# A perceiver layer on one core: x loaded four groups ahead, and stage 3 with its low-rank sums, y norm and splits in another order

## The chip, the cores and the metric

The kernel runs on one core of a Trainium2 chip. The metric is the device time of one execution in microseconds. TensorE is called PE here, VectorE DVE, ScalarE ACT, GpSimd POOL and SyncE SP, as in the rows of the profile.

## The reference

`x` is 128 batches of 32 tokens with 256 channels, `ctx` 128 batches of 257 rows with 256 channels. Three blocks follow each other, each added to `x`:

```
hc = layernorm(x)                                  # cross attention
Sim = hc @ w1 + ctx @ w2 + (hc * w3) @ ctx^T + b;  hq = softmax(Sim) @ ctx
hb = softmax(max_j Sim) @ hc                       # one row per batch
x = x + [hc, hq, hc*hq, hc*hb] @ W_qv + b_qv

z = layernorm(x); xg = z * sigmoid(z @ Wg^T + bg)  # recurrence over the 32 tokens
s = s @ A + xg * Bp;  y = s . Cp + Dp * xg + xg    # state of 16 per channel
x = x + (layernorm(y) * gamma + beta)

n = layernorm(x)                                   # feed-forward, 256 -> 1024 -> 256
h = n @ ternary(w_fc)^T + gate * (n @ v^T @ fast_b^T @ u^T)
x = x + relu(h)^2 @ ternary(w_proj)^T
```

## The kernel before, in words

The 4096 tokens are 32 groups of 128 (four batches each). `resid` holds all of x in SBUF and is updated in place. All instructions of an engine are written out by hand in program order, and engines are held to each other by semaphores (`at_least`, `wait_ge`); there is no scheduler. The program has three blocks.

Stage 1 is a software pipeline over the groups. Its step for group g does three things: part a for group g (turn ctx, scores, softmax), part b for group g - 1 (attention, feature products with `W_qv`), part c for group g - 2 (x sum, second layer norm, `z`, gate, `gated`, which goes to DRAM). `bn`, `mv`, `ve`, `rstd` are the statistics of a layer norm: DVE sums, DVE aggregates, DVE adds epsilon, POOL raises to the power -0.5. In a step DVE first adds the products to x (L843), takes the statistics of that (L848), then waits for x of group g + 1 and takes its statistics (L789, in `layer_norm1`), and only then makes `nmr` (L862) from which ACT makes `z` (L635); ACT then makes `hcwT`, the last two `ctxT` copies (L603) and PE the gate turn (L540) and the scores (L571). SP issues all loads: in step g it waits for `hc_ready`, loads x of group g + 2, waits for PE's attention, loads ctx of group g + 2, stores `gated`, and in every other step loads two groups of gated tokens for the recurrence (`scan_load`). The two semaphores `x_loaded[p]` alternate with the parity of the group.

Stage 2 turns the recurrence into a product with a Toeplitz matrix and prepares the ternary weights; the change does not touch it but for the first y addition. It writes the recurrence's result y to DRAM.

Stage 3 is the feed-forward over 8 chunks of 4 groups (512 tokens). A chunk c has 8 tiles m of 128 hidden units. For a tile PE forms `fc_ps` (L1434, four products of `xn_hi`, which lies in `toeplitz`, and `xn_lo` with `fc_T`, and L1438, one of `lr_parts` with `low_out`), ACT makes `relu` (L1489), DVE squares (L1567, into `scan_x`), ACT takes the high part `sq_hi` (L1497), POOL the low part `sq_lo` (L1526), and three tiles later PE projects both (L1451). `fc_ps` has two buffers, so PE's tile m waits for the square of tile m - 2. In between lies the preparation of later chunks:

- for chunk c + 2: DVE y sums and moments (`y_sums`, `y_moments`, tiles 1 and 2), POOL `neg_mean_y` and `rstd_y` (`lower_y`, `deviation_y`, tile 3), ACT subtracts the mean (`centre_y`, L1008, tile 4), POOL multiplies by gamma (`times_gamma`, L1015, behind tiles 4 and 5), DVE scales and adds to x (`add_y`, L1023, behind tiles 6 and 7). y lies in `y_in` or `below` by the parity of the chunk.
- for chunk c + 1: DVE x sums and moments (tiles 0 and 1), POOL `rstd_x`, `neg_mean_x`, `shift_x` (tile 1), ACT `xn` (`norm_x`, L1058, tiles 2 and 3), PE turns it (`turn_in`, L1417, behind tile 4), ACT `xn_hi` (`split_hi`, tile 5), DVE `xn_lo` (`split_lo`, behind tile 5), PE the low-rank sums (`low_rank`, L1426, behind the hidden tile 7), ACT `lr_hi` (`low_rank_hi`, L1483, behind relu 7), DVE `lr_parts` (`low_rank_parts`, L1559, behind square 7). The product of `lr_parts` in tile 0 of the next chunk waits for it.

At the end of a chunk DVE scales and adds the projection in two halves (`result`, L1575 and L1578), and SP stores 512 tokens (L1404).

## Time and profile before

| | |
|---|---|
| median of 3 runs | 589.56 us (588.4 to 592.37) |
| the profiled execution | 591.37 us |
| its span | 589.6 us |
| PE busy | 501.3 us, 85% of the span |
| DVE busy | 428.4 us, 73% |
| ACT busy | 363.6 us, 62% |
| POOL busy | 334.3 us, 57% |
| the 16 DMA engines, share of hardware queue 1 | 41.5% |

All rows come from one profiled execution. Its span runs from the first to the last event; the execution's own time is 1.8 us longer. Stage 1 lasts to about 344 us, stage 2 to about 401 us, stage 3 to the end.

### The profile page before, as it was taken

What the parts mean: (1) busy time and instruction counts of PE and PEld (TensorE: products, weight loads), DVE (VectorE), ACT (ScalarE), POOL (GpSimd) and SP (SyncE); (2) the same over time, 40 slices, a digit from 0 to 9 for tenths busy, and PEclk for the clock granted to TensorE, in tenths of its full rate; (3) what the DMA queues carried; (4) which work ended last, traced back from release to release, by engine and by line L of the source; (5) the groups of instructions that cost most, each with busy time, mean ns of one, the idle gap of its engine ahead of it and who ended that gap; (6) DMA issues with size and microseconds to landing.
All of it is one profiled execution on the core that took longest, in us unless ns stands there. A gap on an engine that the chain in (4) does not pass through costs nothing. (4 is left out here: it accounts for less than half of the span.)

```text
span 589.6 us, 12951 instructions
## 1 busy us (share of the span) xinstructions
PE 501.3 (85%) x4070; PEld 420.2 (71%) x4070; DVE 428.4 (73%) x1197; ACT 363.6 (62%) x857; POOL 334.3 (57%) x424
## 2 busy tenths in 40 slices
PE   3596999999999999999998716975888988988995
PEld 2375777878787877877786506964777877877884
DVE  2589888888888878887887606943688788788643
ACT  3464767776767766776776405563846846846652
POOL 1488666675757575766665300002767767767653
PEclk9799999999999999999999957995989989989998
DMA  7543365545645475646565761546002202201102
GB/s 225 147 157 100 104 210 156 177 142 175 189 143 176 139 213 131 190 124 205 145 186 149 193 62 39 139 109 148 31 1 72 71 2 73 71 1 36 38 1 71
DMA packets 90035, 69.90 MB, mean 119 GB/s; under 512 B 49504, under 2 KB 73328, under 8 KB 89968
## 3 DMA queue, kind: packets, MB, share of 16 engines
q1 hardware_dynamic: 89968, 69.08, 41.5%
q8 instruction: 33, 0.54, 0.4%
q14 instruction: 34, 0.28, 0.1%
HBM read 55.96 MB, written 13.11 MB: 117 GB/s over the span
## 5 line engine op out<-in xcount | busy, mean ns | idle before, releaser
L1526 POOL TENSOR_TENSOR sq_lo<-scan_x,sq_hi 128x512 fp32r<-128x512 f32 x64 | 83.7, 1308 | 58.5 <-ACT sq_hi L1497 56.5
L1489 ACT ACTIVATE relu<-fc_ps,fc_square 128x512 f32<-128x512 f32 x64 | 43.9, 686 | 54.8 <-PE fc_ps L1438 54.8
L473 PE MATMUL turn_ps<-ident,ctxn 128*128 128x128 f32 x512 | 70.8, 283 | 4.3 <-DMA ctxn<-in_ctx 4.3
L1567 DVE SCALAR_TENSOR_TENSOR scan_x<-fc_ps,relu 128x512 f32<-128x512 f32 x64 | 44.0, 687 | 38.2 <-ACT relu L1489 37.5
L603 ACT COPY ctxT<-turn_ps 128x512 f32<-128x512 f32 x128 | 68.2, 581 | 5.2 <-PE turn_ps L473 5.1
L473 PEld LDWEIGHTS turn_ps<-ident,ctxn 128*128 128x128 f32 x512 | 58.6, 145 | 17.9 <-issue 13.2
L708 POOL TENSOR_TENSOR rstd<-ve,neg_half 128x1 f32<-128x1 f32 x64 | 35.3, 551 | 43.3 <-DVE ve L796 22.5
L722 POOL TENSOR_TENSOR hc_lo<-hc_probT,hc_hi 128x256 fp32r<-128x256 f32 x32 | 23.4, 730 | 56.3 <-ACT hc_hi L610 56.3
L1434 PE MATMUL fc_ps<-toeplitz,fc_T 128*128 128x512 f32 x128 | 54.1, 422 | 0.5 <-DVE scan_x L1567 0.5
L1434 PE MATMUL fc_ps<-xn_lo,fc_T 128*128 128x512 f32 x128 | 53.0, 414 | 0.0
L714 POOL TENSOR_TENSOR proj_in<-proj_in,fc_in 128x512 f32<-128x512 f32 x31 | 49.2, 1588 | 0.0
L1451 PEld LDWEIGHTS proj_ps<-proj_T,sq_hi 128*128 128x128 f32 x256 | 40.5, 195 | 5.4
L1451 PE MATMUL proj_ps<-proj_T,sq_lo 128*128 128x256 f32 x256 | 42.5, 289 | 0.3 <-POOL sq_lo L1526 0.3
L635 ACT ACTIVATE z<-resid,nmr,rstd 128x256 f32<-128x256 f32 x32 | 19.2, 600 | 37.5 <-DVE nmr L862 37.5
L1451 PE MATMUL proj_ps<-proj_T,sq_hi 128*128 128x256 f32 x256 | 41.8, 286 | 0.0
L571 PE MATMUL score_ps<-ctxT,hcwT 128*32 128x257 f32 x512 | 34.8, 389 | 6.9 <-ACT ctxT L603 6.7
L529 PE MATMUL att_ps<-ctxn,hc_probT 128*32 128x256 f32 x512 | 35.1, 393 | 5.4 <-ACT hc_probT L618 5.4
L1497 ACT CAST sq_hi<-scan_x 128x512 fp32r<-128x512 f32 x64 | 39.3, 614 | 0.3 <-DVE scan_x L1567 0.3
L1438 PE MATMUL fc_ps<-lr_parts,low_out 128*128 128x512 f32 x64 | 27.1, 424 | 13.7 <-DVE lr_parts L1559 13.7
L577 PE MATMUL gate_ps<-wgT,zT 128*128 128x256 f32 x128 | 37.0, 413 | 0.5 <-ACT zT L648 0.5
L1451 PEld LDWEIGHTS proj_ps<-proj_T,sq_lo 128*128 128x128 f32 x256 | 36.3, 195 | 0.7 <-POOL sq_lo L1526 0.7
L815 DVE TENSOR_REDUCE fc_in<-proj_in 128x32 f32<-128x512 f32 x31 | 21.2, 685 | 18.5 <-POOL proj_in L714 18.5
(188 smaller groups left out, 1413.3 us busy)
## 6 DMA issues: line engine op xcount, KB each, us to landing
ctxn<-in_ctx SPq DMA_DIRECT2D x32, 1024.0 KB, 5.3
resid<-in_x SPq DMA_DIRECT2D x32, 128.0 KB, 4.7
ctx_end<-in_ctx SPq DMA_DIRECT2D x32, 128.0 KB
gated_tokens<-gated SPq DMA_DIRECT2D x32, 128.0 KB, 5.0
out<-resid SPq DMA_DIRECT2D x8, 512.0 KB, 3.0
scan_x<-gated_tokens SPq DMA_DIRECT2D x60, 64.0 KB, 4.8
scan_tokens<-scan_x SPq DMA_DIRECT2D x4, 768.0 KB, 9.7
y_in<-scan_tokens SPq DMA_DIRECT2D x4, 512.0 KB, 4.4
```

Of the source, the lines that this page charges most:

```text
L473: mm = pe.transpose(turn_ps[b % 2][:, (c * JT + t) * P:(c * JT + t + 1) * P], ctxn[p][:, b, t, c * P:(c + 1) * P], ident[:, :])
L529: mm = pe.matmul(att_ps[b * L:(b + 1) * L, 0:D], hc_probT[p][:, 1, t, b * L:(b + 1) * L], ctxn[o][:, b, t, :], start=(t == 0), stop=(t == ...
L577: mm = pe.matmul(gate_ps[:, 0:D], zT[:, c, :], wgT[:, c, :], start=(c == 0), stop=(c == KD - 1))
L603: act.copy(ctxT[:, b, :, 0:J - 1], turn_ps[b % 2][:, :].rearrange("p (k j) -> p k j", k=KD)).then_inc(ctxT_copied, 1)
L708: pool.tensor_tensor(dst, src, neg_half[:, 0:1], ALU.pow).then_inc(made, 1)
L714: pool.tensor_tensor(v_next[:, :, :, :], a_sb[:, :, :].rearrange("p k (n m) -> p k m n", n=N), state.unsqueeze(2).broadcast_to([P, KD, N, N]),
L1434: pe.matmul(fc_ps[m % 2][:, :], fc_T[:, k, m * P:(m + 1) * P], part[:, c, k, :], start=(k == 0 and i == 0), stop=False)
L1451: mm = pe.matmul(proj_ps[c % 2][r // 2][:, (r % 2) * D:(r % 2 + 1) * D], part[:, m, r * P:(r + 1) * P], proj_T[:, m, :], start=(m == 0 and ...
L1489: act.activation(relu[m % 2], fc_ps[m % 2][:, :], ACT.Relu, scale=fc_square[:, m:m + 1]).then_inc(relu_done, 1)
L1497: act.copy(sq_hi[:, m, :], sq[m % SQ]).then_inc(sq_hi_done, 1)
L1526: pool.tensor_tensor(sq_lo[:, m, :], sq[m % SQ], sq_hi[:, m, :].bitcast(F32), ALU.subtract).then_inc(sq_lo_done, 1)
L1567: dve.scalar_tensor_tensor(out=sq[m % SQ], in0=fc_ps[m % 2][:, :], scalar=0.0, in1=relu[m % 2], op0=ALU.max, op1=ALU.mult).then_inc(sq_don ...
```

## The change

Five edits. In stage 1 x of a group is loaded four groups ahead, on four semaphores in turn. In stage 3: the y norm is done by ACT with scale and shift at once (`norm_y`), for which POOL makes `shift_y` behind `rstd_y`; gamma is multiplied behind that and DVE's addition is a plain sum of 1024 elements in one instruction. The low-rank sums of the next chunk stand ahead of hidden tile 7 on PE, `lr_hi` ahead of relu 7, `xn_lo` ahead of square 5 and `lr_parts` ahead of square 7. Gamma stands ahead of `sq_lo` of tiles 4 and 6, and y's deviation at tile 2. The last tile's projection is done by halves, its `sq_lo` by DVE, and the last chunk is stored in two halves. `x2_done` now counts one per chunk.

```diff
-            x_loaded = [sem(f"x_loaded{p}") for p in range(2)]
+            AHEAD = 4
+            x_loaded = [sem(f"x_loaded{p}") for p in range(AHEAD)]
...
+                    if g + AHEAD < GROUPS:
+                        at_least(sp, hc_ready, g + 1)
+                        load_x(g + AHEAD)
                     if inside or g + 2 < GROUPS:
-                        at_least(sp, hc_ready, g + 1)
-                        load_x(g + 2, p)
                         at_least(sp, attended, g + 1)
...
+                for g in range(2, AHEAD):
+                    load_x(g)
...
-                        at_least(dve, x_loaded[o], sixteen(base, k, -1))
+                        at_least(dve, x_loaded[(g + 1) % AHEAD], 16 * ((g + 1) // AHEAD + 1))
...
         def lower_y(pool, c):
 
-            pool.wait_ge(mv_y_done, c + 1)
-            at_least(pool, yc_done, 2 * c - 2)
+            pool.wait_ge(rstd_y_done, c + 1)
+            at_least(pool, yn_done, 2 * (c - 1))
             pool.tensor_tensor(neg_mean_y[:, :], mv_y[:, :, 0], minus_one[:, :], ALU.mult).then_inc(neg_mean_y_done, 1)
...
+            pool.wait_ge(neg_mean_y_done, c)
+            pool.tensor_tensor(shift_y[:, :], neg_mean_y[:, :], rstd_y[:, :], ALU.mult).then_inc(shift_y_done, 1)
+
+        def norm_y(act, c, h):
+
+            act.wait_ge(shift_y_done, c)
             for r in half(h):
-                ins = act.activation(y_of(c)[:, r, :], y_of(c)[:, r, :], ACT.Identity, bias=neg_mean_y[:, r:r + 1], scale=1.0)
-            ins.then_inc(yc_done, 1)
+                ins = act.activation(y_of(c)[:, r, :], y_of(c)[:, r, :], ACT.Identity, bias=shift_y[:, r:r + 1],
+                                     scale=rstd_y[:, r:r + 1])
+            ins.then_inc(yn_done, 1)
...
-        def add_y(dve, c, h):
-
-            dve.wait_ge(centred, 2 * c + h + 1)
-            dve.wait_ge(rstd_y_done, c + 1)
-            for r in half(h):
-                ins = dve.scalar_tensor_tensor(out=res(c, r), in0=y_of(c)[:, r, :], scalar=rstd_y[:, r:r + 1],
-                                               in1=res(c, r), op0=ALU.mult, op1=ALU.add)
-            ins.then_inc(x2_done, 1)
+        def add_y(dve, c):
+
+            dve.wait_ge(centred, 2 * c + 2)
+            part = resid[:, c * CH:(c + 1) * CH, :]
+            dve.tensor_tensor(part, y_of(c)[:, :, :], part, ALU.add).then_inc(x2_done, 1)
...
+                def project_last(c, m):
+
+                    pe.wait_ge(sq_hi_done, tile(c, m) + 1)
+                    pe.wait_ge(last_lo_done, 1)
+                    for h in range(2):
+                        for part in (sq_hi, sq_lo):
+                            for r in half(h):
+                                mm = pe.matmul(proj_ps[c % 2][h][:, (r % 2) * D:(r % 2 + 1) * D],
+                                               part[:, m, r * P:(r + 1) * P], proj_T[:, m, :],
+                                               start=False, stop=(part is sq_lo), skip_group_check=True)
+                        mm.then_inc(last_half, 1)
...
+                        if m == 7 and has(c, 1):
+                            low_rank(c + 1)
                         if has(c):
                             hidden(c, m)
-                        if m == 7 and has(c, 1):
-                            low_rank(c + 1)
...
+                        if m in (4, 6) and has(c, 2):
+                            times_gamma(pool, c + 2, m // 2 - 2)
+                        if tile(c, m) < CHUNKS * MT - 1:
+                            square_lo(c, m)
...
+                def last_lo(c, m):
+
+                    dve.wait_ge(sq_hi_done, tile(c, m) + 1)
+                    dve.wait_ge(proj_tile, tile(c, m) + 1 - MT)
+                    dve.tensor_tensor(sq_lo[:, m, :], sq[m % SQ], sq_hi[:, m, :].bitcast(F32), ALU.subtract
+                                      ).then_inc(last_lo_done, 1)
```

DVE in chunk 0 of stage 3, from the square of tile 3 to the x sums of the chunk behind, before the change (`scan_x` is the square, `xn_lo` `split_lo`, `resid<-y_in` the y addition):

```order
L1567 SCALAR_TENSOR_TENSOR scan_x<-fc_ps,relu 128x512 x3
L1551 TENSOR_TENSOR xn_lo<-xt_ps,toeplitz 128x512 x2
L1567 SCALAR_TENSOR_TENSOR scan_x<-fc_ps,relu 128x512
L1023 SCALAR_TENSOR_TENSOR resid<-y_in,rstd_y,resid 128x256 x2
L1567 SCALAR_TENSOR_TENSOR scan_x<-fc_ps,relu 128x512
L1559 SCALAR_TENSOR_TENSOR lr_parts<-lr_hi,minus_lo,xt_ps 128x512
L1023 SCALAR_TENSOR_TENSOR resid<-y_in,rstd_y,resid 128x256 x2
L1567 SCALAR_TENSOR_TENSOR scan_x<-fc_ps,relu 128x512
L1032 BN_STATS bn_x<-resid 128x6 x4
```

And now:

```order
L1605 SCALAR_TENSOR_TENSOR scan_x<-fc_ps,relu 128x512 x2
L1589 TENSOR_TENSOR xn_lo<-xt_ps,toeplitz 128x512 x2
L1605 SCALAR_TENSOR_TENSOR scan_x<-fc_ps,relu 128x512 x2
L1597 SCALAR_TENSOR_TENSOR lr_parts<-lr_hi,minus_lo,xt_ps 128x512
L1605 SCALAR_TENSOR_TENSOR scan_x<-fc_ps,relu 128x512
L1040 TENSOR_TENSOR resid<-y_in,resid 128x1024
L1605 SCALAR_TENSOR_TENSOR scan_x<-fc_ps,relu 128x512
L1047 BN_STATS bn_x<-resid 128x6 x4
```

`lr_parts` stood behind half of the y addition and the square of tile 7; it now stands ahead of both, and the whole addition, one instruction, behind the last square.

PE in chunk 0 at hidden tile 7 (`fc_ps`) and the low-rank sums (`xt_ps<-...,low_in`), before:

```order
L1434 MATMUL fc_ps<-toeplitz,fc_T 128x512
L1434 MATMUL fc_ps<-xn_lo,fc_T 128x512
L1434 MATMUL fc_ps<-toeplitz,fc_T 128x512
L1434 MATMUL fc_ps<-xn_lo,fc_T 128x512
L1438 MATMUL fc_ps<-lr_parts,low_out 128x512
L1426 MATMUL xt_ps<-toeplitz,low_in 128x512
L1426 MATMUL xt_ps<-xn_lo,low_in 128x512
L1426 MATMUL xt_ps<-toeplitz,low_in 128x512
L1426 MATMUL xt_ps<-xn_lo,low_in 128x512
L1451 MATMUL proj_ps<-proj_T,sq_hi 128x256 x4
L1451 MATMUL proj_ps<-proj_T,sq_lo 128x256 x4
```

And now:

```order
L1449 MATMUL xt_ps<-toeplitz,low_in 128x512
L1449 MATMUL xt_ps<-xn_lo,low_in 128x512
L1449 MATMUL xt_ps<-toeplitz,low_in 128x512
L1449 MATMUL xt_ps<-xn_lo,low_in 128x512
L1457 MATMUL fc_ps<-toeplitz,fc_T 128x512
L1457 MATMUL fc_ps<-xn_lo,fc_T 128x512
L1457 MATMUL fc_ps<-toeplitz,fc_T 128x512
L1457 MATMUL fc_ps<-xn_lo,fc_T 128x512
L1461 MATMUL fc_ps<-lr_parts,low_out 128x512
L1474 MATMUL proj_ps<-proj_T,sq_hi 128x256 x4
L1474 MATMUL proj_ps<-proj_T,sq_lo 128x256 x4
```

The four sums moved ahead of the tile's five products, so that those and the projection stand between them and the next chunk.

POOL in chunk 0 from `rstd_x` on, before (`sq_lo` is the split of a tile's square, `y_in<-y_in,gamma_all` the gamma product):

```order
L1071 TENSOR_TENSOR rstd_x<-ve_x,neg_half 128x4
L1076 TENSOR_TENSOR neg_mean_x<-mv_x,minus_one 128x4
L1079 TENSOR_TENSOR shift_x<-neg_mean_x,rstd_x 128x4
L1526 TENSOR_TENSOR sq_lo<-scan_x,sq_hi 128x512 x2
L1002 TENSOR_TENSOR neg_mean_y<-mv_y,minus_one 128x4
L1066 TENSOR_TENSOR rstd_y<-ve_y,neg_half 128x4
L1526 TENSOR_TENSOR sq_lo<-scan_x,sq_hi 128x512 x2
L1015 TENSOR_TENSOR y_in<-y_in,gamma_all 128x512
L1526 TENSOR_TENSOR sq_lo<-scan_x,sq_hi 128x512
L1015 TENSOR_TENSOR y_in<-y_in,gamma_all 128x512
L1526 TENSOR_TENSOR sq_lo<-scan_x,sq_hi 128x512 x3
```

And now:

```order
L1087 TENSOR_TENSOR rstd_x<-ve_x,neg_half 128x4
L1092 TENSOR_TENSOR neg_mean_x<-mv_x,minus_one 128x4
L1095 TENSOR_TENSOR shift_x<-neg_mean_x,rstd_x 128x4
L1563 TENSOR_TENSOR sq_lo<-scan_x,sq_hi 128x512
L1082 TENSOR_TENSOR rstd_y<-ve_y,neg_half 128x4
L1017 TENSOR_TENSOR neg_mean_y<-mv_y,minus_one 128x4
L1019 TENSOR_TENSOR shift_y<-neg_mean_y,rstd_y 128x4
L1563 TENSOR_TENSOR sq_lo<-scan_x,sq_hi 128x512 x2
L1033 TENSOR_TENSOR y_in<-y_in,gamma_all 128x512
L1563 TENSOR_TENSOR sq_lo<-scan_x,sq_hi 128x512 x2
L1033 TENSOR_TENSOR y_in<-y_in,gamma_all 128x512
L1563 TENSOR_TENSOR sq_lo<-scan_x,sq_hi 128x512 x3
```

The y statistics moved from ahead of tile 3 to ahead of tile 2 and have a third product; each gamma product moved from behind a tile to ahead of tile 4 and of tile 6.

## Rows read from the trace of the kernel before

**Rows 1.** The page, part 1: busy us, share of span, instructions
```profile
PE 501.3 (85%) x4070; PEld 420.2 (71%) x4070; DVE 428.4 (73%) x1197; ACT 363.6 (62%) x857; POOL 334.3 (57%) x424
```

**Rows 2.** Waits of DVE, 60:345 us: us, times, longest
```profile
DVE bn L789 <- DMA resid<-in_x: 11.4, 13, 1.3
```

**Rows 3.** Timeline, DVE, stage 1, three steps: start us, us, instruction
```profile
154.85 0.42 DVE L843 TENSOR_TENSOR resid<-qv_ps,resid 128x256 f32<-128x256 f32 x1
...
164.79 0.42 DVE L843 TENSOR_TENSOR resid<-qv_ps,resid 128x256 f32<-128x256 f32 x1
...
173.88 0.42 DVE L843 TENSOR_TENSOR resid<-qv_ps,resid 128x256 f32<-128x256 f32 x1
```

**Rows 4.** Timeline, same steps; in brackets idle us before, its releaser
```profile
157.06 0.43 DVE L789 BATCH_NORM_STATS2 bn<-resid 128x6 f32<-128x256 f32 x1 [0.80 <-DMA resid<-in_x]
...
158.78 0.44 PE L540 MATMUL gate_ps<-ident,z 128*128 128x128 f32 x2 [0.29 <-ACT z L635]
...
160.51 1.08 PE L571 MATMUL score_ps<-ctxT,hcwT 128*32 128x257 f32 x16 [0.36 <-ACT ctxT L603]
...
168.49 1.05 ACT L603 COPY ctxT<-turn_ps 128x512 f32<-128x512 f32 x2
...
169.59 1.07 PE L571 MATMUL score_ps<-ctxT,hcwT 128*32 128x257 f32 x16
```

**Rows 5.** Waits of PE, 375 to 590 us
```profile
PE fc_ps L1438 <- DVE lr_parts L1559: 13.7, 6, 2.3
...
PE xt_ps L1417 <- ACT xn L1058: 1.5, 3, 1.1
```

**Rows 6.** Timeline, stage 3, end of a chunk, 515 to 521 us
```profile
515.86 1.29 POOL L1526 TENSOR_TENSOR sq_lo<-scan_x,sq_hi 128x512 fp32r<-128x512 f32 x1
...
515.93 2.92 DVE L1023 SCALAR_TENSOR_TENSOR resid<-y_in,rstd_y,resid 128x256 f32<-128x256 f32 x2 [0.66 <-POOL y_in L1015]
...
516.04 0.59 ACT L1483 CAST lr_hi<-xt_ps 128x512 fp32r<-128x512 f32 x1 [0.27 <-PE xt_ps L1426]
...
517.12 1.45 POOL L1015 TENSOR_TENSOR y_in<-y_in,gamma_all 128x512 f32<-128x512 f32 x1
...
519.38 0.73 DVE L1559 SCALAR_TENSOR_TENSOR lr_parts<-lr_hi,minus_lo,xt_ps 128x512 fp32r<-128x512 f32 x1
...
520.17 0.50 PE L1438 MATMUL fc_ps<-lr_parts,low_out 128*128 128x512 f32 x1 [2.29 <-DVE lr_parts L1559]
```

**Rows 7.** Windows: us, busy PE, PEld, DVE, ACT, POOL, clock, DMA
```profile
431.50:435.50 4.00, 4.00 (x18) 3.52 (x18) 2.22 (x6) 1.78 (x3) 1.29 (x1) 0.57 0.00 0
453.00:475.60 22.60, 19.27 (x117) 16.70 (x117) 18.98 (x40) 14.39 (x27) 16.22 (x16) 1.00 0.16 47
543.60:548.20 4.60, 4.60 (x22) 4.09 (x22) 2.92 (x8) 2.38 (x4) 1.28 (x1) 0.63 0.02 4
548.20:580.00 31.80, 31.80 (x200) 28.56 (x200) 17.95 (x31) 20.27 (x36) 19.47 (x17) 1.00 0.10 34
```

**Rows 8.** The page, part 6: loads of x, KB each, us to landing
```profile
resid<-in_x SPq DMA_DIRECT2D x32, 128.0 KB, 4.7
```

**Rows 9.** Durations min/median/max of the y addition; group of the result's sum
```profile
L1023 DVE SCALAR_TENSOR_TENSOR resid<-y_in,rstd_y,resid x16: 472/480/1508, 382.8 to 520.4; 128x256 f32<-128x256 f32 x16
...
L1578 DVE TENSOR_TENSOR resid<-proj_ps,resid 128x512 f32<-128x512 f32 x16 | 11.1, 692 | 0.5
```

**Rows 10.** Timeline, PE, product of lr_parts, tile 0, chunks 4, 6, 7
```profile
498.53 0.50 PE L1438 MATMUL fc_ps<-lr_parts,low_out 128*128 128x512 f32 x1 [2.28 <-DVE lr_parts L1559]
...
543.31 0.50 PE L1438 MATMUL fc_ps<-lr_parts,low_out 128*128 128x512 f32 x1 [2.27 <-DVE lr_parts L1559]
...
563.66 0.40 PE L1438 MATMUL fc_ps<-lr_parts,low_out 128*128 128x512 f32 x1
```

**Rows 11.** Timeline, POOL and DVE at the end
```profile
580.11 2.53 POOL L1526 TENSOR_TENSOR sq_lo<-scan_x,sq_hi 128x512 fp32r<-128x512 f32 x2 [0.81 <-ACT sq_hi L1497]
...
583.46 0.70 DVE L1575 TENSOR_TENSOR proj_ps<-proj_ps,proj_scale_all 128x512 f32<-128x512 f32 x1 [3.21 <-PE proj_ps L1451]
```

More of the change, by code:

```diff
@@ L1332, in _ @@
                 centre_first(dve)
-                for h in range(2):
-                    add_y(dve, 0, h)
+                add_first(dve)
                 x_sums(dve, 0)
@@ L1401, in _ @@
                         load_y(c + 2)
-                    if has(c, -1):
+                    if 1 <= c < CHUNKS:
                         at_least(sp, out_ready, 2 * c)
@@ L1506, in _ @@
                             split_hi(c + 1)
+                        if m == 7 and has(c, 1):
+                            low_rank_hi(c + 1)
                         if has(c):
                             relu_tile(c, m)
-                        if m == 7 and has(c, 1):
-                            low_rank_hi(c + 1)
                         if m >= 1 and has(c):
@@ L1516, in _ @@
                             norm_x(act, c + 1, m - 2)
-                        if m == 4 and has(c, 2):
-                            for h in range(2):
-                                centre_y(act, c + 2, h)
+                        if m in (4, 5) and has(c, 2):
+                            norm_y(act, c + 2, m - 4)
             @block.gpsimd
@@ L1578, in result @@
                     dve.tensor_tensor(part, bank, part, ALU.add).then_inc(out_ready, 1)
+                def last_lo(c, m):
[3 more added lines that the diff above has]
+                                      ).then_inc(last_lo_done, 1)
                 split_lo(0)
                 low_rank_parts(0)
-                for h in range(2):
-                    add_y(dve, 1, h)
+                add_y(dve, 1)
                 for c in range(CHUNKS + 1):
                     for m in range(MT):
+                        if m == 5 and has(c, 1):
+                            split_lo(c + 1)
+                        if m == 7 and has(c, 1):
+                            low_rank_parts(c + 1)
                         if has(c):
```

73 lines of the change are left out of this document (45 added, 28 removed).

## The prediction

> **What bounds the kernel now.** I read the page's busy line first, then the waits of each engine by stage, then the timelines round the longest of them. PE is busy for 85% of the span and no other engine for more than 73% [rows 1], so the question in each stage is which wait stops PE. Two kinds matter here, one in stage 1 and one in stage 3.
>
> Stage 1. The vector engine waits 13 times for an x group that is still in flight, 11.4 us together, longest 1.3 us [rows 2]. The reader is to see whether that is paid for. A group without such a wait goes from one `resid` sum to the next in 173.88 - 164.79 = 9.09 us; the one before it, with a wait of 0.80 us, takes 164.79 - 154.85 = 9.94 us [rows 3, 4]. So 0.80 us of waiting costs 0.85 us. The way is visible: the wait sits ahead of the small operations that ScalarE's `z` needs, PE then stands 0.29 us for `z` and 0.36 us for `ctxT`. In the free group ScalarE's last `ctxT` pair ends at 168.49 + 1.05 = 169.54 and PE starts the scores at 169.59, so the ScalarE chain has no slack even there, and a delay on it goes through in full [rows 4].
>
> Stage 3. PE waits six times for `lr_parts`, 13.7 us together, and three times for `xn`, 1.5 us together [rows 5]. One of the six, step by step [rows 6]: ScalarE takes the low-rank sums at 516.04. With 0.59 us for that and 0.73 us for `lr_parts` the parts could be there at 517.4, before PE asks for them at 520.17 - 2.29 = 517.88. But VectorE has started the first half of the y addition at 515.93, and that pair takes 2.92 us, because GpSimd runs `sq_lo` from 515.86 and the gamma product from 517.12; then comes a square; `lr_parts` starts only at 519.38. After four of the six gaps PE's granted clock falls from its 2.4 GHz level to 1.2 GHz for some 4 us: means of 0.57 over 4.0 us at the first and 0.63 over 4.6 us at the last [rows 7]. After the other two it stays at 1.00.
>
> **The change, part by part.**
>
> x four groups ahead. SyncE issues as many loads as before; x of groups 2 and 3 is issued two steps earlier at the start, in a stretch where its queue next waits for PE anyway, and later groups three steps before they are read. A step is 9 us long and one load lands in 4.7 us [rows 8], so nothing is left of the 13 waits. No engine's order changes. By rows 3 the wait goes through at 0.85 for 0.80, so the term is **-11.4 us**. Bounds: -7, if the alternate groups hold another short wait that now shows; -12 at the other end. What is late next is the chain through `z` and `ctxT`, whose period is the 9.09 us.
>
> Low-rank sums earlier, the y addition behind them. PE now forms the sums ahead of the last hidden tile; ScalarE takes them ahead of its relu; VectorE makes `lr_parts` ahead of the square and of the y addition. By the times above the parts would have been ready at 517.4 even in the old PE order, and PE now has a whole hidden tile more in between. The six gaps go: **-13.7 us**. If the cover were gone (VectorE late by over 1.5 us) part of a gap returns.
>
> The clock. Each fall loses about (1 - 0.57) x 4.0 = 1.7 us or (1 - 0.63) x 4.6 = 1.7 us of PE work [rows 7]. What PE did before each fall was to stand for the 2.3 us of a gap; from 548.2 to 580, where no gap occurs, the clock stays at 1.00 [rows 7]. With the gaps gone I take back 4 x 1.55, a little under the loss, since part of the slow stretch lets the other engines catch up: **-6.2 us** (bounds 0 and -6.8).
>
> y norm on ScalarE with both factors. The four ScalarE instructions stay four; their scale is now the deviation instead of 1.0, and I take the same duration. They stand in two halves, one ahead of `split_hi` and one behind it, so that `split_hi` comes two instructions earlier. GpSimd has one more product of 4 elements per chunk, and its gamma products stand ahead of `sq_lo` of tiles 4 and 6. The sums allow this: the gamma product takes about 1.4 us [rows 6], and PE reads `sq_lo` of a tile three tiles (over 6 us) later.
>
> The y addition. Four instructions of 472 to 480 ns undisturbed and up to 1508 ns beside GpSimd [rows 9] become one of 1024 elements. The trace has none of that shape. A VectorE sum of 512 elements takes 692 ns [rows 9]; twice that, 1.4 us, is the top for the instruction alone, and 1.1 us (twice, less a fixed part) the bottom; I take 1.25. It also can meet a GpSimd instruction: of the pair in rows 6 each addition waited for a GpSimd instruction to end, then ran. The new one can wait so once, up to 1.3 us, against twice or more before. In the old program the gap on PE gave VectorE time to catch up after it; now it starts the new chunk 19.3 us after the last one and the addition stands ahead of the first square. Walking VectorE's list for one chunk, the addition ends about 0.9 us after the first relu result is ready, the x sums and moments follow 0.3 to 0.7 us later than now relative to the tiles, and with them `shift_x`, and `xn`, for which PE already waits at the turn [rows 5]. I price that at 0.35 us a chunk: **+2.1 us** over six. Bounds: -3.9, if even the present small waits go (the chunk without y work takes 563.66 - 543.31 = 20.35 us, less 1.7 us of slow clock 18.65 us, against 520.17 - 498.53 - 2.29 = 19.35 us in the free part of a chunk with it [rows 6, 10]; 0.65 x 6 = 3.9); and +8, a lag of 1.3 us a chunk.
>
> On such collisions the Trainium skill (SBUF — State Buffer, section Who interferes with whom) says that a VectorE instruction with two SBUF inputs and a GpSimd instruction that reads SBUF exclude each other for their whole length. The 1508 ns against 472 ns agree. By that rule one long addition is one meeting instead of up to four, but GpSimd stands for all of it if it comes second; the sum would be the same, since `sq_lo` has the slack named above, and the upper bound is the case in which both meet every chunk.
>
> The last chunk. `sq_lo` of the last tile moves from GpSimd, where two run back to back from 580.11 to 582.64 [rows 11], to VectorE: about 0.7 us instead of 1.3, after the first of them. The results now start when half of the last products is there, and the first half is stored while the second is computed. Now VectorE starts the result at 583.46 [rows 11]; I expect 582.7, and about 0.3 us less for the smaller last store: **-1.0 us** (bounds 0 and -2).
>
> Stage 3's start (the first y addition as one instruction, GpSimd's two small ones swapped) lies beside PE's first tiles: 0, between -0.5 and +0.5.
>
> Sum: -11.4 - 13.7 - 6.2 + 2.1 - 1.0 = -30.2 us. The profiled execution took 591.37 us, 1.8 us over its span of 589.6, so 561.2 by that execution. It stands 1.8 us over the median of the three runs, 589.56; against the median I say **559.4 us**.
>
> **The rivals.**
>
> A. VectorE, or its meetings with GpSimd, takes the place of the gap in stage 3. For it: VectorE is busy 18.98 us in a stretch of 22.60 [rows 7], and its list shrinks by less than 1 us while the chunk is to shrink to about 19.7 us; an addition that meets GpSimd each time costs up to 2.5 us. Against it: much of those 18.98 us is itself waiting behind GpSimd, and a square may be over 1 us late before PE notices. Price: 1.3 us a chunk, and two of the four slow stretches stay: +0.95 x 6 + 2 x 1.55 = +8.8, so 568.
>
> B. In stage 1 only half of the waiting is regained, because in the alternate groups, where SyncE also stores and loads scan data, something else ends 0.4 us later. For it: the 9.09 and 9.94 us alternate, so the two kinds of group differ in more than the wait. Against it: 0.80 us of wait explains the 0.85. Price +5.7: 565.
>
> C. Slower. GpSimd works in order, and its deviation of y now stands ahead of `sq_lo` of tile 2 and waits for VectorE's y moments, its gamma products ahead of `sq_lo` of tiles 4 and 6 wait for ScalarE. If these three engines come to wait for each other in a ring, `sq_lo` comes late for PE in every chunk. A chunk takes (543.31 - 498.53) / 2 = 22.4 us now [rows 10]. To end over 1% slower, stage 3 must give back the 12.4 us of the x loads and the last chunk and 5.9 us more, 3.05 us a chunk over six: it decides from 25.5 us a chunk. With 26 us the time is 589.6 - 12.4 + 6 x 3.6 = 599. Against it: each of those inputs is ready 1 to 3 us before GpSimd reaches it by the walk.
>
> D. The low-rank sums are in time but PE's clock falls all the same, at the turn. Against it: the turn's waits now, up to 1.1 us, are not followed by a fall. Price +6.2: 565.6.
>
> **How the numbers follow.** Forecast 0.62 (its own range 555 to 564), A 0.14, B 0.11, D 0.06, C 0.02, and 0.05 for more than the sum, down to 552 (the low ends of the x lag and the clock). The range 554 to 570 leaves out part of A, C and the far low end. A measurement of this kernel tells about 1% from no change. Faster by over 1% (under 583.7): 0.96, all but C and the far end of A; within: 0.02, that far end; slower: 0.02, C.
>
> **What would show it.** Right: no wait of the bn of stage 1 for x after the first group; groups all near 9.1 us; no PE wait for `lr_parts`; chunks of 19.4 to 20 us from the product of `lr_parts` in tile 0 of one to that of the next; clock 1.00 from the second tile of stage 3 to the last; `lr_parts` within 1 us of `lr_hi`. The lag term is right if PE's wait at the turn grows by some 0.3 us a chunk. Wrong: groups of 9.5 us without x waits (B); PE waits in the middle of chunks for squares, or VectorE busy over 95% of a chunk (A); waits for `sq_lo` (C); a granted clock of 0.5 behind the turn (D).

## The result, and the profile after

| | before | after |
|---|---|---|
| median, us | 590.84 (588.4 to 592.37, 4 runs) | 560.0 (557.7 to 561.19, 4 runs) |
| profiled execution | 591.37 | 557.7 |
| its span | 589.6 | 555.9 |

The ratio is 0.9477, 95% interval 0.9428 to 0.9526: about 30.8 us faster. The forecast was 559.4 us. Its sum for the profiled execution was 561.2, and that execution took 557.7. Executions far from the others of their kernel (two of run 5, 808 and 1196 us, one of the kernel before beside runs 9 to 12, 951 us, and the longest of run 9, 583 us) are counted as slow and left out of every ratio.

The page of the changed kernel, its busy line and the granted clock in 40 slices of the span:

```profile
PE 491.9 (88%) x4070; PEld 417.1 (75%) x4070; DVE 415.0 (75%) x1177; ACT 365.4 (66%) x857; POOL 334.9 (60%) x430
...
PEclk9799999999999999999999985899699999999999
```

and the clock line of the kernel before:

```profile
PEclk9799999999999999999999957995989989989998
```

PE is busy 9.4 us less [rows 1], with the same 4070 instructions. Stage 3 is the last dozen slices of either line. Before, four of them stand at 8. Three (the 30th, 33rd and 36th) are falls behind a gap; the fourth fall, from 543.6 us on [rows 7], lies across the 37th and 38th and leaves both at 9, and the 40th is the end of the kernel. After, none stands under 9 behind the stage's start.

Stage 1: DVE's sum of x at the ends of one step.

```profile
151.41 0.42 DVE L848 TENSOR_TENSOR resid<-qv_ps,resid 128x256 f32<-128x256 f32 x1
...
160.53 0.42 DVE L848 TENSOR_TENSOR resid<-qv_ps,resid 128x256 f32<-128x256 f32 x1
```

From 55 to 345 us DVE's waits hold none for x, where [rows 2] had 11.4 us. A step takes 160.53 - 151.41 = 9.12 us, the period of the step without a wait in [rows 3]; the step of 9.94 us is gone.

Stage 3: waits of PE, 385 to 556 us.

```profile
PE xt_ps L1440 <- PEq L1100: 5.8, 1, 5.8
...
PE xt_ps L1440 <- ACT xn L1073: 0.7, 1, 0.7
```

No wait for `lr_parts` is left, those for squares are 0.8 us in all, and the one for `xn` [rows 5] is a single one, in the first chunk. The end of a chunk, to be held against [rows 6]:

```profile
452.17 0.59 ACT L1521 CAST lr_hi<-xt_ps 128x512 fp32r<-128x512 f32 x1
...
452.79 0.75 DVE L1597 SCALAR_TENSOR_TENSOR lr_parts<-lr_hi,minus_lo,xt_ps 128x512 fp32r<-128x512 f32 x1 [0.53 <-ACT lr_hi L1521]
...
454.62 1.32 POOL L1563 TENSOR_TENSOR sq_lo<-scan_x,sq_hi 128x512 fp32r<-128x512 f32 x1
454.71 2.31 DVE L1040 TENSOR_TENSOR resid<-y_in,resid 128x1024 f32<-128x1024 f32 x1
...
455.01 0.40 PE L1461 MATMUL fc_ps<-lr_parts,low_out 128*128 128x512 f32 x1
```

`lr_parts` starts 0.62 us after `lr_hi` (3.34 us before), ends at 453.54 and is read at 455.01, with no bracket: PE did not wait. The y addition, now one instruction, starts behind `lr_parts` and runs past PE's product without touching it. It takes 2.31 us, because `sq_lo` has started 0.09 us ahead of it; alone it takes 1.22 us, the smallest of its group's durations (min/median/max):

```profile
L1040 DVE TENSOR_TENSOR resid<-below,resid x4: 1219/2307/2307, 398.5 to 511.9; 128x1024 f32<-128x1024 f32 x4
```

Windows of stage 3 from its first chunk to its last tile (us, busy us of PE, PEld, DVE, ACT, POOL, granted clock, DMA share, GB/s), to be held against [rows 7]:

```profile
409.00:440.00 31.00, 30.87 (x189) 27.23 (x188) 24.49 (x48) 23.84 (x44) 24.98 (x24) 1.00 0.11 35
...
460.00:549.00 89.00, 88.34 (x547) 78.04 (x545) 65.66 (x129) 64.84 (x117) 66.81 (x66) 1.00 0.13 42
```

The clock stays at 2.4 GHz in both, and PE is busy 99% of them. The starts of `lr_parts` from chunk to chunk lie 19.07 us apart (433.73, 452.79, 471.86, 490.93, 509.99).

Three places split the 33.7 us between the spans. PE's first turn of stage 3, and its product of `lr_parts` in tile 0 of the last chunk:

```profile
390.60 1.73 PE L1440 MATMUL xt_ps<-ident,xn 128*128 128x128 f32 x7 [5.81 <-PEq L1100]
...
531.28 0.40 PE L1461 MATMUL fc_ps<-lr_parts,low_out 128*128 128x512 f32 x1
```

The first stood at 401.39 before:

```profile
401.39 1.94 PE L1417 MATMUL xt_ps<-ident,xn 128*128 128x128 f32 x8 [5.89 <-PEq L1084]
```

and the second at 563.66 [rows 10]. So 10.8 us come from stages 1 and 2, (563.66 - 401.39) - (531.28 - 390.60) = 162.3 - 140.7 = 21.6 us from seven chunks of stage 3, and 1.3 us from the end.

### The profile page after: what moved, and what is told of

It is laid out like the page before. It is cut to its first block and busy times, and to the rows that moved or that the text cites. A ratio compares the mean times of both kernels' runs of the same rounds, so it can differ in the third digit from the quotient of the medians.

```text
span 555.9 us, 12923 instructions
## 1 busy us (share of the span) xinstructions
PE 491.9 (88%) x4070; PEld 417.1 (75%) x4070; DVE 415.0 (75%) x1177; ACT 365.4 (66%) x857; POOL 334.9 (60%) x430
## 5 line engine op out<-in xcount | busy, mean ns | idle before, releaser
L1563 POOL TENSOR_TENSOR sq_lo<-scan_x,sq_hi 128x512 fp32r<-128x512 f32 x63 | 83.1, 1319 | 33.7 <-ACT sq_hi L1535 33.7
L1457 PE MATMUL fc_ps<-toeplitz,fc_T 128*128 128x512 f32 x128 | 52.1, 407 | 0.8 <-DVE scan_x L1605 0.8
L1457 PE MATMUL fc_ps<-xn_lo,fc_T 128*128 128x512 f32 x128 | 51.0, 398 | 0.0
L1474 PEld LDWEIGHTS proj_ps<-proj_T,sq_hi 128*128 128x128 f32 x252 | 38.5, 188 | 5.7
L1474 PE MATMUL proj_ps<-proj_T,sq_lo 128*128 128x256 f32 x252 | 40.1, 281 | 0.3 <-POOL sq_lo L1563 0.3
L1474 PE MATMUL proj_ps<-proj_T,sq_hi 128*128 128x256 f32 x252 | 40.1, 281 | 0.0
L1474 PEld LDWEIGHTS proj_ps<-proj_T,sq_lo 128*128 128x128 f32 x252 | 34.2, 188 | 0.5 <-POOL sq_lo L1563 0.5
L676 ACT ACTIVATE prob<-score_ps,neg_max 128x257 f32<-128x257 f32 x32 | 15.3, 477 | 28.8 <-DVE neg_max L902 28.8
```

What stands on the lines that cost most here:

```text
L1457: pe.matmul(fc_ps[m % 2][:, :], fc_T[:, k, m * P:(m + 1) * P], part[:, c, k, :], start=(k == 0 and i == 0), stop=False)
L1474: mm = pe.matmul(proj_ps[c % 2][r // 2][:, (r % 2) * D:(r % 2 + 1) * D], part[:, m, r * P:(r + 1) * P], proj_T[:, m, :], start=(m == 0 and ...
L1563: pool.tensor_tensor(sq_lo[:, m, :], sq[m % SQ], sq_hi[:, m, :].bitcast(F32), ALU.subtract).then_inc(sq_lo_done, 1)
```

## The experiments

Twelve kernels on three chips: runs 1 to 4 on one, 5 to 8 on the second, 9 to 12 on the third. Each ratio is to the kernel before on the same chip. "The changed kernel" is the one with the whole change.

**1. x alone.** The kernel before with the x loads of the change, nothing else:

```diff
-            x_loaded = [sem(f"x_loaded{p}") for p in range(2)]
+            AHEAD = 4
+            x_loaded = [sem(f"x_loaded{p}") for p in range(AHEAD)]
...
+                    if g + AHEAD < GROUPS:
+                        at_least(sp, hc_ready, g + 1)
+                        load_x(g + AHEAD)
                     if inside or g + 2 < GROUPS:
-                        at_least(sp, hc_ready, g + 1)
-                        load_x(g + 2, p)
...
```

> The kernel before with the x loads four groups ahead and nothing else. My theory (each of the 13 waits for x is paid by PE in full): 11 us less than before, 0.981 of it, stage 1 ends 11 us sooner, all groups 9.1 us, stage 3 as before with six waits of 2.3 us for lr_parts. Rival B (something else holds the alternate groups): 5 to 6 us less, 0.990.

Measured: 579.42 us, ratio 0.9762 (0.9713 to 0.9811). DVE's waits for x are gone, PE's for `lr_parts` are all there (13.6 us, 6 times). By the medians that is 14.0 us, 3 more than my theory said; by the trace the last x sum of stage 1 comes 10.4 us earlier (327.57 against 337.95), which is what the theory priced. The rest is not traced: three of the six gaps are followed by a fall of the clock here, four in the kernel before.

**2. Stage 3 alone.** The changed kernel with the x loads as before.

> The changed kernel with the x loads as before. My theory: the two parts add up, so about 19 us less than before, 0.967, with the 13 waits for x back. Rival (the parts help each other, because a shift in time moves the clock's falls): this and the run with x alone add up to clearly more or less than the whole change's 30 us.

Measured: 571.07 us, ratio 0.9635 (0.9563 to 0.9707). The waits for x are back, 12.0 us in 13; no wait for `lr_parts`. So 14.0 us for the first part and 22.4 for the second on this chip (before: 593.47), where I had 19 for the second. Their sum of 36.4 stands beside 33.2 for the kernel of run 4, which has nearly the whole change, and 30.8 for the change itself. The two intervals leave some 5 us of room, so the parts add up or nearly so; a small loss in putting them together isn't ruled out.

**3. Only the low-rank sums moved.** x ahead, the new low-rank order on PE, ACT and DVE, but the y addition as before, in four scaled instructions between the squares.

```diff
+                        if m == 5 and has(c, 1):
+                            split_lo(c + 1)
+                        if m == 7 and has(c, 1):
+                            low_rank_parts(c + 1)
                         if has(c):
                             square(c, m)
```

> The kernel before with the x loads ahead and the new order of the low-rank sums and splits on PE, ACT and DVE; the y norm, gamma and the y addition in two halves behind tiles 6 and 7 stay. Theory 1 (the first half of the y addition holds lr_parts, wherever the low-rank sums stand): lr_parts still comes behind a pair of 2.9 us, PE still waits for it, 1.6 us a chunk instead of 2.3, and clock falls remain: 570 to 577 us, 0.966 to 0.977. Theory 2 (the new order of the sums is what removes the gap): 561 to 563 us, 0.952.

**4. Only the y norm and addition moved.** The changed kernel with PE, ACT and DVE's low-rank steps back behind hidden tile, relu and square.

> The changed kernel with the low-rank sums, lr_hi, lr_parts and xn_lo back in their old places, so that only the y norm and the y addition have moved. Theory 1: lr_parts is ready at 516.04 + 0.59 + 0.73 = 517.4 by the old trace's times against 517.88 when PE asks, so no gap and the same time as the changed kernel within 1 us, 0.948 to 0.951. Theory 2 (the new order is what counts): gaps of over 1 us and 570 us or more.

Measured: run 3 572.98 us, ratio 0.9656 (0.9619 to 0.9692); run 4 560.26 us, ratio 0.9439 (0.9387 to 0.9491). In run 3 PE's wait, and what stands ahead of `lr_parts` on DVE:

```profile
PE fc_ps L1442 <- DVE lr_parts L1563: 10.1, 6, 1.7
```

```profile
460.79 2.92 DVE L1027 SCALAR_TENSOR_TENSOR resid<-y_in,rstd_y,resid 128x256 f32<-128x256 f32 x2 [1.23 <-POOL y_in L1019]
463.64 0.73 DVE L1563 SCALAR_TENSOR_TENSOR lr_parts<-lr_hi,minus_lo,xt_ps 128x512 fp32r<-128x512 f32 x1
```

In run 4 the same place:

```profile
455.52 0.75 DVE L1597 SCALAR_TENSOR_TENSOR lr_parts<-lr_hi,minus_lo,xt_ps 128x512 fp32r<-128x512 f32 x1
456.29 2.31 DVE L1040 TENSOR_TENSOR resid<-y_in,resid 128x1024 f32<-128x1024 f32 x1
```

The y addition in front of `lr_parts` was the gap; moved behind it, the gap is gone even with the old low-rank order, and the time is that of the whole change. The new low-rank order alone makes each gap 0.6 us shorter and, beside the moved addition, brings nothing that can be measured. Run 4 moves y's norm, gamma and addition together. That it is the addition's place is read from DVE's list, and run 9 bears it out; whether the norm had to move to ACT for it, no run tells.

**5. The changed kernel again**, on the chip of runs 6 to 8, so that these have it beside them.

> The changed kernel once more, to stand beside the next three on one chip: 0.945 to 0.951 of before.

Measured: two executions count, 556.13 and 563.45 us, ratio 0.944 (0.9339 to 0.9541), so the interval is wide.

**6. The y addition in four.** The changed kernel, its sum of 1024 as four of 256, in the same place:

```diff
-            dve.tensor_tensor(part, y_of(c)[:, :, :], part, ALU.add).then_inc(x2_done, 1)
+            for r in range(CH):
+                ins = dve.tensor_tensor(res(c, r), y_of(c)[:, r, :], res(c, r), ALU.add)
+            ins.then_inc(x2_done, 1)
```

> The changed kernel with the y addition as four sums of 256 elements instead of one of 1024. In the changed kernel the one sum takes 2.31 us where it meets sq_lo and 1.22 us where it does not, and PE never waits for it. My theory (PE bounds the chunk, VectorE has slack): the same time within 1 us; the four may take longer together, 1.7 us and up. Theory 2 (one meeting instead of several is what the change lives on): 3 us or more slower, chunks above 19.07 us.

Measured: 567.20 us, ratio 0.9564 (0.9517 to 0.9612), 7 us over the 560.0 of the changed kernel. The intervals just overlap, so the trace has to carry the point: its chunks are longer by 1.18 us, 7.1 us in six. My expectation fell, theory 2 held. DVE and POOL at one of the places, and PE's waits:

```profile
438.47 1.30 POOL L1564 TENSOR_TENSOR sq_lo<-scan_x,sq_hi 128x512 fp32r<-128x512 f32 x1
438.54 3.65 DVE L1040 TENSOR_TENSOR resid<-below,resid 128x256 f32<-128x256 f32 x4
440.54 1.37 POOL L1564 TENSOR_TENSOR sq_lo<-scan_x,sq_hi 128x512 fp32r<-128x512 f32 x1 [0.77 <-ACT sq_hi L1536]
```

```profile
PE fc_ps L1458 <- DVE scan_x L1606: 4.0, 8, 0.6
PE xt_ps L1441 <- ACT xn L1074: 3.9, 7, 0.7
```

Away from GpSimd the four took 1.42 us, the one takes 1.22; beside it 3.65 against 2.31, since four sums last long enough to meet a second `sq_lo`. DVE so has 1.34 us more a chunk, and the chunk goes from 19.07 to 20.25 us (the starts of `lr_parts` go from 416.37 to 537.88 in six chunks): 1.18 of the 1.34 come through. PE now waits at the turn (`xn`) and for squares, as the prediction's rival A had it. In the changed kernel PE is the bound, but DVE stands only some 0.2 us a chunk behind it.

**7 and 8. The last scan store out of stage 2.** In the changed kernel PE waits 5.8 us at the start of stage 3, where the block of stage 2 ends only when SP has issued its last stores. Run 7 issues them in stage 3's list instead; run 8 also has the y norm of the third chunk one or two tiles later.

Run 7's edit:

```diff
-                sp.wait_ge(scan_copied, SCANS)
-                store_scan(scan_x, EARLY, BATCH - EARLY, y_stored3)
...
+                sp.wait_ge(scan_copied, SCANS)
+                for q in range(NB):
...
+                    sp.dma_start(dst, scan_x[q * L:(q + 1) * L, EARLY:BATCH, :]).then_inc(y_stored3, 16)
                 sp.wait_ge(y_stored3, 16 * NB)
```

> The changed kernel with the last four stores of the recurrence's result issued in stage 3's SyncE list instead of stage 2's. In the changed kernel PE stands 5.8 us at the start of stage 3 while SyncE issues those stores for 11.8 us. My theory: PE starts 5.8 us sooner, but y of chunk 2 still lands at 400.4 us, while VectorE would ask for it at 396.5, so VectorE and then PE wait some 3 to 4 us in chunk 0: 2 us faster than the changed kernel. Rival: PE waits for the recurrence stores themselves and nothing is gained.

> As the last, and in chunk 0 alone the y preparation of chunk 2 stands two tiles later on VectorE, GpSimd and ScalarE. My theory: the wait for y in chunk 0 goes as well, 4 to 5.8 us faster than the changed kernel. Rival: no better than the last.

Measured: 565.42 us, ratio 0.954 (0.9491 to 0.959), and 562.08 us, ratio 0.9494 (0.9425 to 0.9563): no gain in either. In run 7 SP issues the four stores for 11.8 us, and the load of y stands behind them:

```profile
388.44 11.81 SPq L1417 DMA_DIRECT2D scan_tokens<-scan_x  x4
406.35 0.38 SPq L1410 DMA_DIRECT2D y_in<-scan_tokens  x1
```

```profile
DVE bn_y L979 <- DMA y_in<-scan_tokens: 9.4, 1, 9.4
```

PE's wait at the start of the stage falls from 5.8 to 0.9 us, as expected, but the wait for y is 9.4 us in run 7 and 6.3 in run 8. My theory had 3 to 4 and none, with y landing at 400.4 as in the changed kernel. It left out that the stores, once in stage 3's list, start only when stage 2 is over: at 388.44 us instead of 378.39, and the load of y stands behind them.

**9. The gap put back.** The changed kernel, in which PE's product of `lr_parts` also waits for the y addition, as the queue of before made it do:

```diff
                         at_least(pe, lr_done, c + 1)
+                        at_least(pe, x2_done, min(c + 2, CHUNKS) if c else 0)
```

> The changed kernel, in which TensorE's first product of each chunk's low-rank correction also waits for VectorE's y addition of the next chunk (as the queue of the kernel before made it do without saying so). In the changed kernel the low-rank sums end 2.2 us before TensorE wants them and the addition (2.31 us) ends about 2 us after that. Theory 1 (the gap is what cost, and a halt is followed by a fall of the granted clock, as in the kernel before): PE waits about 2 us in each of six chunks, 12 us, and some of the gaps are followed by a stretch of granted clock under 1.0, up to 1.7 us each; the time is 574 to 582 us, ratio 0.97 to 0.985. Theory 2 (a halt of 2 us is too short to bring the clock down, the kernel before fell for another reason): the clock line stays at 9 through stage 3, the time is 571 to 574, ratio about 0.968.

Measured: 577.69 us, ratio 0.974 (0.9692 to 0.9788), as theory 1 had it. The rows are of its longest execution, 583.24 us; it stood 6.6 us longer between stages 1 and 2 than the changed kernel (last section), which is outside the rows used here. PE's wait, and four of its products one chunk apart:

```profile
PE fc_ps L1462 <- DVE resid L1040: 11.8, 6, 2.0
```

```profile
427.52 0.47 PE L1462 MATMUL fc_ps<-lr_parts,low_out 128*128 128x512 f32 x1 [1.99 <-DVE resid L1040]
...
450.34 0.47 PE L1462 MATMUL fc_ps<-lr_parts,low_out 128*128 128x512 f32 x1 [1.99 <-DVE resid L1040]
...
472.65 0.47 PE L1462 MATMUL fc_ps<-lr_parts,low_out 128*128 128x512 f32 x1 [1.95 <-DVE resid L1040]
...
493.95 0.47 PE L1462 MATMUL fc_ps<-lr_parts,low_out 128*128 128x512 f32 x1 [1.99 <-DVE resid L1040]
```

```profile
426.50:431.50 5.00, 3.98 (x15) 3.54 (x16) 2.87 (x6) 1.19 (x2) 1.29 (x1) 0.66 0.00 0
```

The clock is back to falling, behind the gaps at 427.52, 450.34 and 515.25 us and not behind those at 472.65 and 493.95. A chunk whose gap is followed by no fall takes 493.95 - 472.65 = 21.30 us; the three with a fall take 22.82, 22.31 and 22.42, so a fall costs 1.0 to 1.5 us here. Against the 19.07 of the changed kernel a gap of 1.99 us costs 2.23. The falls are a consequence of the gap. In run 3, with gaps of 1.7 us, the chunks show none. Why some gaps of 2 us are followed by a fall and others not, the runs don't settle.

**10. Two groups ahead, in another order.** The kernel before, x still on two semaphores, but its load ahead of the scan's loads in SP's list:

```diff
...
+                    next_x(base + 1)
                     if not isinstance(base, int) or base >= 4:
                         scan_load_pair(base)
                     step(base + 1, 0, ())
```

> The kernel before, with x still two groups ahead on two semaphores, but in SyncE's list the next x load stands ahead of the eight loads of the scan's tokens instead of behind them. Theory 1 (x was late only because those issues, about 2.1 us each other group, stood ahead of it): VectorE's waits for x after 55 us are gone as in the run with x alone four ahead, ratio 0.976 to 0.982. Theory 2 (two groups ahead is too short in any order, since the buffer comes free only then): waits of 0.24 us or more stay in each other group, ratio 0.985 to 0.99.

Measured: 580.95 us, ratio 0.9827 (0.9776 to 0.9877). SP's list in the kernel before and here:

```profile
150.15 2.14 SPq L180 DMA_DIRECT2D scan_x<-gated_tokens  x4
152.33 0.45 SPq L362 DMA_DIRECT2D resid<-in_x  x1
```

```profile
146.59 0.47 SPq L362 DMA_DIRECT2D resid<-in_x  x1
147.16 1.97 SPq L180 DMA_DIRECT2D scan_x<-gated_tokens  x4
```

```profile
DVE bn L797 <- DMA resid<-in_x: 0.2, 1, 0.2
```

The last line is all that is left of the 13 waits, and the last x sum of stage 1 starts at 326.4 us, as early as in the changed kernel (327.0). So two groups ahead was enough; x was late because 2.1 us of issues stood in front of its load. The ratio lies just outside what theory 1 had, while the median is only 1.5 us over that of run 1 (579.42), on another chip; the two are not told apart. The profiled execution, 585.78 us, is the longest of the four, and there PE stood 19.7 us between stages 1 and 2, against 13.0 in run 1 (last section); for the other three no trace tells.

**11. The last chunk as before.**

```diff
-                            if c == CHUNKS and m == BEHIND - 1:
-                                project_last(c - 1, MT - 1)
-                            else:
-                                project(c - 1, MT - BEHIND + m)
+                            project(c - 1, MT - BEHIND + m)
```

with its `sq_lo` on GpSimd and one store again.

> The changed kernel with the last chunk as before: one projection order, one low split of the last squares on GpSimd, one store. Theory 1 (the edit is worth what the prediction took, about 1 us, 1.4 by the two traces): from the start of the last ReLU to the end of the span 10.5 to 10.9 us instead of 9.35, ratio 0.950. Theory 2 (the shorter tail of the changed kernel came from the chunk's new order, not from this edit): the stretch stays at 9.3 to 9.6 us.

Measured: 561.66 us, ratio 0.9503 (0.9456 to 0.955). The edit is too small for the ratio to tell, but not for the trace. DVE's first and last step of the result in this run, then in the changed kernel:

```profile
553.09 0.70 DVE L1603 TENSOR_TENSOR proj_ps<-proj_ps,proj_scale_all 128x512 f32<-128x512 f32 x1 [3.24 <-PE proj_ps L1468]
...
555.16 0.69 DVE L1606 TENSOR_TENSOR resid<-proj_ps,resid 128x512 f32<-128x512 f32 x1
```

```profile
550.57 0.70 DVE L1616 TENSOR_TENSOR proj_ps<-proj_ps,proj_scale_all 128x512 f32<-128x512 f32 x1 [0.90 <-PE proj_ps L1487]
...
552.64 0.69 DVE L1619 TENSOR_TENSOR resid<-proj_ps,resid 128x512 f32<-128x512 f32 x1
```

From the start of the last relu (548.44 here, 546.55 there) to the result 4.65 against 4.02 us, and from its end to the end of the span 559.2 - 555.85 = 3.35 against 555.9 - 553.33 = 2.57 us: 0.6 us by the halves of the projection, 0.8 by the smaller store, 1.4 together. From the last relu to the end of the span it is 10.76 us against 9.35, as theory 1 had it.

**12. The last scan store in two parts.** As run 7, but the 16 batches of the third chunk are stored first, then that chunk's y is loaded, then the other 80 batches are stored:

```diff
+                store_late(EARLY, EARLY + CH * NB, y_stored3)
+                sp.wait_ge(y_stored3, 16 * NB)
                 for c in range(CHUNKS + 1):
                     if has(c, 2):
                         load_y(c + 2)
+                    if c == 0:
+                        store_late(EARLY + CH * NB, BATCH, y_stored4)
+                        sp.wait_ge(y_stored4, 16 * NB)
```

> The changed kernel, in which the last store of the scan's tokens is issued in stage 3's list instead of at the end of stage 2, in two parts: the 16 batches of the third chunk first (four stores of 128 KB), the load of that chunk's y behind them, then the other 80 batches. The two runs that moved the store whole lost TensorE's 5.8 us wait at the stage's start but got a wait of 9.4 or 6.3 us for y. Theory 1 (only y's lateness stood against it): TensorE's first turn of stage 3 comes about 5 us earlier and y of the third chunk lands before VectorE asks for it; time 552 to 557, ratio 0.935 to 0.943. Theory 2 (the gain is taken again by another wait in the stage's first chunk): the wait for y is gone but the time stays at 558 to 562.

Measured: 554.14 us (550.98 to 558.0, 6 runs), ratio 0.9371 (0.9326 to 0.9415), against 0.9477 (0.9428 to 0.9526) for the changed kernel at first and 0.944 (0.9339 to 0.9541) in run 5. It stands clear of the first interval and inside the second, which is wide, and neither was taken on this chip; so those two don't settle it. Run 11 was taken on this chip: 561.66 us, interval 0.9456 to 0.955, clear of this one. It lacks the last-chunk edit, worth 1.4 us, which leaves about 6 us for the store. The way of the gain is in the trace:

```profile
385.66 1.98 SPq L1420 DMA_DIRECT2D scan_tokens<-scan_x  x4
389.56 0.38 SPq L1411 DMA_DIRECT2D y_in<-scan_tokens  x1
389.98 10.45 SPq L1420 DMA_DIRECT2D scan_tokens<-scan_x  x4
```

```profile
385.71 1.06 PE L1451 MATMUL xt_ps<-ident,xn 128*128 128x128 f32 x8 [0.93 <-PEq L1101]
```

y is asked for at 389.56, where run 7 asked at 406.35 and the changed kernel at 396.10. No wait for it is left, and the first turn stands at 385.71 instead of the changed kernel's 390.60. The span is 550.2 us, 5.7 under that of the changed kernel. Theory 1 held, and this is the fastest version of the study.

## Why the prediction was right, point by point

Held against the two profiled executions the terms come out so, in us:

| term | predicted | in the traces |
|---|---|---|
| x ahead | -11.4 | -10.8 |
| the six gaps | -13.7 | -13.7 |
| the clock | -6.2 | -5.5 |
| the lag of VectorE, six chunks | +2.1 | -2.4 |
| the last chunk | -1.0 | -1.3 |
| sum | -30.2 | -33.7 |

The sum missed by 3.5 us. That the median of 560.0 stands only 0.6 us from the forecast of 559.4 is in part luck: the profiled execution of the changed kernel is the fastest of its four, 2.3 us under their median, and that hides most of the miss.

**x ahead, -11.4: right.** The last x sum of stage 1 comes 10.96 us earlier (326.99 against 337.95), the first turn of stage 3 10.8 us earlier. Run 1 shows it alone. Rival B (half of it) is out: from 60 us on, all steps but the last few are 9.1 us or, three of them, 9.5. That four groups ahead were needed was not claimed, and run 10 shows that they were not.

**The six gaps, -13.7: right in size, half right in reason.** I gave the low-rank sums, moved earlier, and the addition, moved behind, together as the cause. Runs 3 and 4 separate them: the addition's move is enough by itself, and without it 10.1 of the 13.7 us stay. The step of the prediction that held was the one that read VectorE's queue in [rows 6]: the parts could have been ready at 517.4 even in the old PE order.

**The clock, -6.2: right, and now tested.** From the second tile of stage 3 on it stays at 2.4 GHz, which refutes rival D, and run 9 shows that forced gaps bring the falls back. What the falls cost can be read from the kernel before. Two more of its products of `lr_parts`:

```profile
453.89 0.50 PE L1438 MATMUL fc_ps<-lr_parts,low_out 128*128 128x512 f32 x1 [2.29 <-DVE lr_parts L1559]
...
475.51 0.50 PE L1438 MATMUL fc_ps<-lr_parts,low_out 128*128 128x512 f32 x1 [2.27 <-DVE lr_parts L1559]
```

A chunk without a fall takes 475.51 - 453.89 = 21.62 us, one with a fall 498.53 - 475.51 = 23.02 [rows 10]. The other two with y work and a fall take 22.91 and 23.14, and the last, without y work, 20.35 against 19.07 now. That makes 1.3 to 1.5 us a fall, 5.5 for the four.

**The lag of VectorE, +2.1: wrong in sign.** This is the step that failed: "I price that at 0.35 us a chunk". The walk itself was right as far as it went. The addition ends 0.9 us after the first relu, and the x sums start 0.66 us later, counted from the product of `lr_parts`: at 457.55 - 455.01 = 2.54 us against 500.40 - 498.53 = 1.87. But the walk went down VectorE's list alone. Before and now, in the chunks that start at 498.53 and at 455.01:

```profile
500.40 1.40 DVE L1032 BATCH_NORM_STATS2 bn_x<-resid 128x6 f32<-128x256 f32 x4
...
502.46 1.29 POOL L1526 TENSOR_TENSOR sq_lo<-scan_x,sq_hi 128x512 fp32r<-128x512 f32 x1 [0.82 <-ACT sq_hi L1497]
...
502.92 0.86 DVE L1045 TENSOR_SCALAR ve_x<-mv_x 128x4 f32<-128x4 f32 x1
```

```profile
457.55 1.39 DVE L1047 BATCH_NORM_STATS2 bn_x<-resid 128x6 f32<-128x256 f32 x4
...
458.84 1.30 POOL L1563 TENSOR_TENSOR sq_lo<-scan_x,sq_hi 128x512 fp32r<-128x512 f32 x1 [0.66 <-ACT sq_hi L1535]
...
459.85 0.32 DVE L1060 TENSOR_SCALAR ve_x<-mv_x 128x4 f32<-128x4 f32 x1
```

`rstd_x`, the next step, is GpSimd's and stands behind that `sq_lo` in its list. It starts 0.1 us behind its end both times, at 503.85 and 460.25. And `ve_x`, which takes 0.17 us at its shortest, ends 0.03 us behind the same `sq_lo`, whether it started early and took 0.86 us or late and took 0.32. So GpSimd's split set the time, VectorE's lag vanished behind it, and `xn` comes 0.1 us earlier than before. PE had no slack to give: the turn starts 0.05 us behind the end of `xn` in either kernel. In run 6 the x sums start 3.85 us behind the product, `ve_x` ends 0.4 us behind the `sq_lo`, and the turn waits. That is the lag as I had priced it, once it is larger than what GpSimd hides.

A chunk takes 19.07 us against the 19.35 of its free part before; that is -1.4 in the five full chunks, and the first one is 1.0 us shorter than its gap explains. Of the 0.28 us a chunk some 0.16 belongs to the gap: by my estimate from the trace before, PE's products start 0.24 us apart but last 0.40, so a product that had not waited would have started 0.16 us before the idle time began. Of the first chunk's 1.0 us 0.4 is a shorter wait for `xn`, 0.75 us against 1.12; the rest was not traced. The term's bounds (-3.9 to +8) held it. The lower one has a slip: 19.35 - 18.65 is 0.70, not 0.65, so it should be -4.2.

The value of 1.25 us for the addition alone was right (1.22). How close the other end was shows run 6: with 1.34 us more on VectorE a chunk costs 1.18 us more, and the time is 567.2, where rival A said 568. So the mechanism of A is real; it was kept out by the single long instruction.

**What the meeting with GpSimd is.** In the trace the addition started 0.09 us behind a `sq_lo` of 1.32 us and took 2.31 us: the rest of `sq_lo` (1.23) and its own 1.22 make 2.45. The rule of the Trainium skill that the prediction weighed (SBUF — State Buffer, section Who interferes with whom) agrees here to 0.14 us. The prediction left its sum unchanged for that rule, since `sq_lo` has slack. That was right for GpSimd's side; run 6 shows what the number of meetings is worth on VectorE's, because a further meeting is up to another `sq_lo`'s length on the engine that has little time to spare.

**The last chunk, -1.0: right**, 1.3 by the traces and 1.4 by run 11. I had the halves at 0.7 and the store at 0.3; they are 0.6 and 0.8.

**Stage 3's start and the y norm, 0: right.** From the first turn of the stage to its first product of `lr_parts` it is 8.07 us in both kernels. ScalarE's y norm takes 603 to 606 ns instead of the 504 to 507 of the subtraction, against the assumed same duration; 0.1 us four times a chunk, on an engine with room, shows nowhere. Rival C, the ring of waits through GpSimd, did not come about: PE's waits for `sq_lo` are 0.3 us in all.

## What to carry to other kernels

When PE waits for a small result, look at what stands ahead of it in the queue of the engine that makes it: moving one long neighbour behind it gave more here than making the result earlier. Give a load its place ahead of the long issues in its queue before you give it more buffers, and split a long store where a load waits behind it. Where two engines collide, fewer and longer instructions on the one without time to spare met the other less often here; test that slack with a deliberate surplus before counting on it. And when you walk one engine's list to price a delay, follow it to the next engine: what stands ahead there may hide it.
